# Sequence stage: four of 32 products with B moved from VectorE to GpSimd, their decays computed in place in PSUM

## What is computed

```
xi, z = split(seq @ in_proj)
xc    = silu(conv1d(xi) + b)
dt, Bm, Cm = split(xc @ x_proj);  dt = softplus(dt * dt_proj_w + dt_proj_b)
A   = -exp(A_log)
dA  = exp(dt[..., None] * A)
dBx = dt[..., None] * Bm[:, :, None, :] * xc[..., None]
h   = dA_t * h + dBx_t            (8 steps, h0 = 0)
y_t = sum_n h * C_t               ys + D * xc, times silu(z), then out_proj
```

## Time and profile before

| | us |
|---|---|
| median of three runs (10599.95 to 10654.83) | 10605.33 |
| the profiled execution | 10650.4 |
| its span | 10648.6 |
| VectorE busy in the span | 8923.8 (84%) |
| TensorE busy | 8596.3 (81%) |
| ScalarE busy | 6268.9 (59%) |
| GpSimd busy | 6010.0 (56%) |

### The profile page before, as it was taken

One profiled execution on the slowest core, in us unless ns is written; L12 is line 12 of the kernel. 1 busy time (PEld: TensorE's weight loads), 2 busy tenths in 40 slices (PEclk: granted clock), 3 DMA queues, 4 the chain that ended last, 5 costly groups with the idle time before them and its releaser, 6 DMA issues. The chain is left out here.

```text
span 10648.6 us, 196346 instructions
## 1 busy us (share of the span) xinstructions
PE 8596.3 (81%) x61658; PEld 3647.3 (34%) x61658; DVE 8923.8 (84%) x10968; ACT 6268.9 (59%) x11797; POOL 6010.0 (56%) x3646
## 2 busy tenths in 40 slices
PE   6999999989999997787877777877877777777760
PEld 3555555555555553222222222222222222222210
DVE  7777777777777775999999999999999999999984
ACT  5666666666666664555555555555555555555543
POOL 3222222222222221878878878787778878778760
PEclk9999999999999998888888888898888888888875
DMA  2223322232332321111111111111111111111129
GB/s 67 68 68 75 73 68 68 72 78 74 74 75 73 76 73 39 37 33 37 37 33 37 37 33 38 36 33 39 34 33 39 35 33 41 33 35 39 33 49 266
DMA packets 855791, 591.00 MB, mean 56 GB/s; under 512 B 621424, under 2 KB 725872, under 8 KB 848464
## 3 DMA queue, kind: packets, MB, share of 16 engines
q1 hardware_dynamic: 751440, 423.61, 17.3%
q0 software_dynamic: 49152, 100.76, 2.6%
q10 hardware_dynamic: 54016, 51.91, 1.6%
HBM read 109.27 MB, written 103.81 MB: 20 GB/s over the span
## 5 line engine op out<-in xcount | busy, mean ns | idle before, releaser
L1190 POOL TENSOR_TENSOR b_hh<-b_hh,b_cn 128x1024 f32<-128x1024 f32 x1600 | 3834.4, 2414 | 1053.3 <-DVE b_hh L1445 1052.9
L1445 DVE TENSOR_TENSOR_SCAN b_hh<-b_dA,b_ub 128x512 f32<-128x512 f32 x3200 | 3865.7, 1208 | 0.0
L1314 ACT ACTIVATE b_dA<-b_db,b_negA 128x448 f32<-128x448 f32 x3200 | 1980.6, 634 | 1761.4 <-PE b_db L1539 1755.4
L278 POOL DMA_DIRECT2D kvsel<-kv x1536 | 1104.2, 721 | 2877.1 <-issue 2456.0
L1437 DVE TENSOR_TENSOR b_ub<-b_ub,b_bn 128x512 f32<-128x512 f32 x3200 | 2174.8, 680 | 378.2 <-PE b_ub L1539 358.3
L1539 PE MATMUL b_ub<-b_rows,b_pick 96*64 96x512 bf16 x6400 | 1405.1, 440 | 1008.2 <-DVE b_hh L1445 949.8
L1539 PEld LDWEIGHTS b_ub<-b_rows,b_pick 96*64 96x64 bf16 x6400 | 359.1, 110 | 3194.7 <-DVE b_hh L1445 2535.5
L1539 PE MATMUL b_db<-b_rows,b_pick 96*64 96x512 bf16 x6400 | 1267.2, 419 | 218.7 <-ACT b_dA L1314 214.7
L554 DVE SCALAR_TENSOR_TENSOR oacc<-vpad,vec,oacc 128x1064 f32<-128x1064 f32 (+1 forms) x934 | 1199.4, 1301 | 11.4
L1575 PE MATMUL b_acc<-b_hh,b_gather 64*32 64x512 f32 x12800 | 1050.7, 719 | 2.8 <-POOL b_hh L1190 2.8
L395 ACT ACTIVATE prob<-score,nmax 128x256 f32<-128x256 f32 (+1 forms) x1600 | 737.4, 479 | 161.0 <-issue 91.3
(11 more groups left out here) (185 smaller groups left out, 12247.5 us busy)
## 6 DMA issues: line engine op xcount, KB each, us to landing
b_rows<-b_term SPq DMA_DIRECT2D x2400, 64.0 KB, 2.0
kvsel<-kv SPq DMA_DIRECT2D x1600, 64.0 KB, 2.1
kvsel<-kv POOLq DMA_DIRECT2D x1536, 64.0 KB
xpad<-in_x SPq DMA_DIRECT2D x18, 1568.0 KB, 10.7
ys<-ysb ACTq DMA_DIRECT2D x16, 1600.0 KB, 9.4
b_yc<-ys SPq DMA_DIRECT2D x100, 256.0 KB, 2.7
xr<-b_xo SPq DMA_DIRECT2D x100, 256.0 KB, 2.7
x<-x3pad SPq DMA_DIRECT2D x16, 1568.0 KB, 18.2
```

What stands on the lines that cost most here:

```text
L278: eng.dma_start(kvsel[:, slot, j, :, WPIX * t:WPIX * (t + 1)].unsqueeze(1), kv[:, bass.ds(at[t], 1), :, :]).then_inc((s_kv, s_kg)[j][slot] ...
L1190: nc.gpsimd.tensor_tensor(out=now, in0=now, in1=cn[:, par, :].unsqueeze(1).broadcast_to([C, 2, HT]), op=ALU.mult).then_inc(s_pm, 1)
L1314: nc.scalar.activation(later(dA[:, k % DEEP, :]), later(db[k % 2][:, :]), ACT.Exp, scale=negA[:, 8 * q + e:8 * q + e + 1]).then_inc(s_a, 1)
L1445: nc.vector.tensor_tensor_scan(hh[:, k // 2 % PDEEP, HT * (k % 2):HT * (k % 2 + 1)], dA[:, k % DEEP, :], ub[(UNITS * par + k) % 3][:, :], ...
```

## The change

Units 24, 26, 28 and 30 of each chunk are handled in another way (`AHEAD`). TensorE puts dt into their bank `ub` and u into `db`, the reverse of the others. ScalarE copies u from `db` to a place of the unit's own in SBUF (`su`), where GpSimd multiplies it with B (before pairs 8, 9, 10 and 11 of its products with C). ScalarE then makes the decay in place in PSUM: a copy of zeros into column t = 0 of `ub`, and an exponential over the other seven. These two stand in ScalarE's order after the decays of units 29, 31, 33 and 35 (the last two are units 1 and 3 of the next chunk). VectorE's scan of such a unit takes the rates from `ub` and the new terms from `su`, and has no product before it. The semaphore `bk` now counts 28 products in a chunk; `ex` and `sb` are new.

```diff
+        AHEAD = (24, 26, 28, 30)
+        PLAIN = UNITS - len(AHEAD)
+        su = sb("su", [C, len(AHEAD), HT])
...
+            def states_in(n, par, k):
+                pool.wait_ge(s_a, unit(n, k))
+                pool.wait_ge(s_bn, ONE + 2 * n + 1)
+                nc.gpsimd.tensor_tensor(out=own(k), in0=own(k), in1=bn[:, par, :], op=ALU.mult).then_inc(s_sb, 1)
...
                 for j in range(PAIRS):
+                    for k in AHEAD:
+                        if (k - 7) // 2 == j:
+                            states_in(n, par, k)
                     products(n, par, j)
...
             def decay(n, k):
                 act.wait_ge(s_dr, unit(n, k))
+                if k in AHEAD:
+                    if not is_first(n):
+                        act.wait_ge(s_sc, unit(n - 1, k))
+                    nc.scalar.activation(own(k), db[k % 2][:, :], ACT.Copy).then_inc(s_a, 1)
+                    return
...
+            def decay_in_place(n, par, k):
+                act.wait_ge(s_ur, unit(n, k))
+                q, e = channel(k)
+                here = ub[(UNITS * par + k) % 3][:, :]
+                nc.scalar.activation(first_of(here), first_of(dA[:, 0, :]), ACT.Copy)
+                nc.scalar.activation(later(here), later(here), ACT.Exp, scale=negA[:, 8 * q + e:8 * q + e + 1]
+                                     ).then_inc(s_ex, 1)
...
                 for k in range(28, 32):
                     decay(n, k)
+                    if k == 29:
+                        decay_in_place(n, par, 24)
+                    if k == 31:
+                        decay_in_place(n, par, 26)
                 if before_end(n, 2):
                     turned(n + 2)
                 if more:
-                    for k in range(UNITS, UNITS + LEAD):
+                    decay(n, UNITS)
+                    decay(n, UNITS + 1)
+                decay_in_place(n, par, 28)
+                if more:
+                    for k in range(UNITS + 2, UNITS + 4):
+                        decay(n, k)
+                decay_in_place(n, par, 30)
+                if more:
+                    for k in range(UNITS + 4, UNITS + LEAD):
                         decay(n, k)
...
             def recur(n, par, k):
-                dve.wait_ge(s_bk, unit(n, k))
-                dve.wait_ge(s_a, unit(n, k))
+                here = ub[(UNITS * par + k) % 3][:, :]
+                if k in AHEAD:
+                    dve.wait_ge(s_ex, ahead(n, k))
+                    dve.wait_ge(s_sb, ahead(n, k))
+                    rate, new = here, own(k)
+                else:
+                    dve.wait_ge(s_bk, plain(n, k))
+                    dve.wait_ge(s_a, unit(n, k))
+                    rate, new = dA[:, k % DEEP, :], here
...
-                    if k + 1 < UNITS or more:
+                    if k + 1 not in AHEAD and (k + 1 < UNITS or more):
                         states_in(n, par, k + 1)
                     recur(n, par, k)
...
-                repeat(ub[(UNITS * par + k) % 3], 1, par, k, s_ur)
+                repeat(ub[(UNITS * par + k) % 3], 0 if k in AHEAD else 1, par, k, s_ur)
...
-                repeat(db[k % 2], 0, par, k, s_dr)
+                repeat(db[k % 2], 1 if k in AHEAD else 0, par, k, s_dr)
```

More of the change, by code:

```diff
@@ L1050, in sequences @@
         s_sc = sem("sc")
+        s_ex = sem("ex")
+        s_sb = sem("sb")
         s_pm = sem("pm")
@@ L1077, in unit, with plain, ahead, own @@
             return ONE + UNITS * n + k + 1
+        def plain(n, k):
+            q, r = divmod(k, UNITS)
+            return ONE + PLAIN * n + PLAIN * q + len([x for x in range(r + 1) if x not in AHEAD])
+        def ahead(n, k):
+            return ONE + len(AHEAD) * n + AHEAD.index(k) + 1
+        def own(k):
+            return su[:, AHEAD.index(k), :]
         def pair(n, j):
@@ L1100, in later, with first_of @@
             return x.rearrange("c (m t) -> c m t", t=T)[:, :, 1:T]
+        def first_of(x):
+            return x.rearrange("c (m t) -> c m t", t=T)[:, :, 0:1]
         block = ctx.enter_context(nc.Block())
@@ L1130, in split @@
                     if r == 0 and not is_first(n):
-                        sp.wait_ge((s_dr, s_ur)[x], ONE + UNITS * n - UNITS)
+                        sp.wait_ge(s_dr, ONE + UNITS * n - UNITS)
+                        sp.wait_ge(s_ur, ONE + UNITS * n - UNITS)
                     for q in range(Q):
@@ L1295, in kept @@
                 if not early(n, 3):
-                    act.wait_ge((s_bk, s_pm)[x], ONE + (UNITS, PAIRS)[x] * n - 2 * (UNITS, PAIRS)[x])
+                    act.wait_ge((s_bk, s_pm)[x], ONE + (PLAIN, PAIRS)[x] * n - 2 * (PLAIN, PAIRS)[x])
+                    if x == 0:
+                        act.wait_ge(s_sb, ONE + len(AHEAD) * n - 2 * len(AHEAD))
                 nc.scalar.activation((bn, cn)[x][:, par, :], misc[:, :], ACT.Copy).then_inc(s_bn, 1)
@@ L1440, in recur @@
             def recur(n, par, k):
-                dve.wait_ge(s_bk, unit(n, k))
-                dve.wait_ge(s_a, unit(n, k))
+                here = ub[(UNITS * par + k) % 3][:, :]
[7 more added lines that the diff above has]
+                    rate, new = dA[:, k % DEEP, :], here
                 if k % 4 == 0 and not (is_first(n) and k // 2 < PDEEP):
                     dve.wait_ge(s_y, quad(n, (k // 2 - PDEEP) // 2))
-                nc.vector.tensor_tensor_scan(hh[:, k // 2 % PDEEP, HT * (k % 2):HT * (k % 2 + 1)], dA[:, k % DEEP, :],
-                                             ub[(UNITS * par + k) % 3][:, :], 0.0, ALU.mult, ALU.add
-                                             ).then_inc(s_sc, 1)
+                nc.vector.tensor_tensor_scan(hh[:, k // 2 % PDEEP, HT * (k % 2):HT * (k % 2 + 1)], rate, new, 0.0,
+                                             ALU.mult, ALU.add).then_inc(s_sc, 1)
             front(0)
```

## The result

| | before | after |
|---|---|---|
| median us | 10610.51 (4 runs) | 10546.53 (4 runs, 10544.08 to 10566.67) |
| ratio after / before, 95% interval | | 0.9936 [0.9918, 0.9955] |
| span of the profiled execution | 10648.6 | 10564.6 |
| mean granted clock | 0.898 | 0.899 |
| distance from the `gate` of one chunk to the next, mean of 93 chunks | 61.23 | 60.58 |

Ratios and medians leave out two timed executions that took over 17000 us, one of e9 and one of the kernel before beside e5 to e7.

The account below looks back on a forecast made before the run. VectorE was taken to bound the chunk as a whole, TensorE the stretch of units 24 to 30. 0.65 us x 100 chunks = 65 us gave about 10585 profiled, 10540 us as median; range 10430 to 10665.

Parts of the forecast that it names:

- TensorE is the bound from u25 to u31: In units 24 to 30 TensorE is as long as VectorE or longer, so the 2.32 us off VectorE mostly doesn't count.
- p31 and s30 come 0.65 us earlier on average: Behind u31, product 31 and scan 30 come forward 0.53, 0.67 and 0.75 us in three chunks, 65 us over 100 chunks.
- 1.67 us of new waiting per chunk: Of the 2.32 us VectorE saves per chunk in this stretch, 0.65 is gained and 1.67 becomes waiting.
- The in-place pair costs 0.72 us and delays `conv_even`: ScalarE's zero copy and exponential ahead of the yT copy take 0.72 us, delaying conv_even 0.01, 0.72, 0.25 us in three chunks.
- The scans at 1.21 us with rates from PSUM, the register instruction free, GpSimd covered: VectorE's four scans stay at 1.21 us, the added register instructions cost nothing, GpSimd's 4.8 us per chunk fits its waits.
- The rule against the change: Two-input elementwise work belongs on VectorE; alone it would make 4.8 us of GpSimd work for 2.3, set aside.
- The clock: TensorE's granted clock, left unchanged in the sum; rivals had it stay up more (17%) or fall once more per round (14%).
- the rivals: TensorE's clock stays up more, 106 us gained (17%), or falls once more per round, 86 us lost (14%).
- the first rival: TensorE's waits behind u31 shrink, so its clock falls less often: another 106 us gained, 10434 us, chance 17%.
- units 15 to 22: Units before u25 in which TensorE was called idle, given as evidence against the clock staying up more (17%).
- T's sums: Forecasts per run from the theory that TensorE's stretch from u25 to u31 sets when scan 30 can start.
- The prediction's sentence on the rule of the clock page: Idleness throttles TensorE and activity frees it; said to support the clock staying up more, 106 us, chance 17%.

Follow-up runs that it names:

- e9: Kernel before with units 22, 28 and 30 handled in the new way: 0.9787 of the kernel before, 10387.47 us.
- e5: Kernel before, no unit in the new way, transposes moved from s = 24 to 19, conv_even to 20, 21, 22, ScalarE's copies likewise: 0.9996 of the kernel before.
- e7: Changed kernel with only unit 30 handled in the new way: 0.9914 of the kernel before.
- e2: Changed kernel with only units 28 and 30 handled in the new way: 0.9879 of the kernel before.
- e8: Changed kernel with only unit 22 in the new way, its decay in place behind decay 27: 0.9954 of the kernel before.
- e3: Changed kernel with only units 24 and 26 handled in the new way: 0.9993 of the kernel before.
- e0: The changed kernel run again, no edit: 0.9945 of the kernel before.
- e1: Changed kernel with the copy to yT moved ahead of the decay in place of unit 26: 0.9890 of the kernel before.
- e6: Changed kernel with transposes, conv_even and ScalarE's two copies moved earlier as in e5: 0.9931 of the kernel before.
- e10: Units 20, 22, 28 and 30 in the new way, that is e9 plus unit 20: 0.9845 of the kernel before.
- e4b: Changed kernel with one more ScalarE copy of 512 columns just ahead of the copy to yT: 0.9934 of the kernel before.
- e11: The same kernel as e9 run again for a trace: 0.9798 of the kernel before, 10396.01 us.

## Why the prediction was right, point by point

- **TensorE is the bound from u25 to u31.** Right, and shown: products behind the stretch (e2, e7) or ahead of it (e8) count, those inside it (e3) do not, and this holds between chunks of like clock too.
- **p31 and s30 come 0.65 us earlier on average.** Right at like clock: 0.52 us where the level is low (0.53 was said for such a chunk) and 0.70 us at the middle clock (0.75 was said). Not so on average: in the trace of the change s30 comes 0.09 us earlier behind s22 than before, in that of e0 0.35 us, because the clock from u25 to u31 fell from 0.734 to 0.675 and 0.694. The mean chunk is 0.65 us shorter all the same, because the clock behind u31 rose, which gives 0.64 us. That the two came to the forecast is luck.
- **1.67 us of new waiting per chunk.** 170 us in the trace, but of two parts: VectorE's waits for units 24 to 31 grew by 2.3 us per chunk, and those further on fell by 0.6.
- **The in-place pair costs 0.72 us and delays `conv_even`.** 0.73 us measured. From u25 to u31 the delay is none at the lower level (14.25 us before and after; 0.01 was said) and 0.21 us at the middle clock (11.10 for 10.89; 0.25 was said). Moving the pair behind the copy (e1) brings some 60 us where 28 were priced; the rest goes with the clock (0.906 for 0.902).
- **The scans at 1.21 us with rates from PSUM, the register instruction free, GpSimd covered.** Right: 1212 ns; VectorE busy 54.9 us in a chunk (55.3 was said); 1268 ns per product of GpSimd where 1.2 us was taken, and the `add` hardly waits for it: TensorE waits 3.0 us for GpSimd in all.
- **The rule against the change** (the Trainium skill, GPSIMD Engine Reference, Engine selection): a product does take 1268 ns for 680 ns, a ratio of 1.9 where the page says about 2, and by it alone the change would lose. It does not, because GpSimd's waits fell by 557 us. The price shows in e6, where TensorE no longer covers it, and in e10, one product beyond e9: there GpSimd is the one waited for.
- **The clock.** The sum left it at zero, and the rivals had it gain 106 us or lose 86. Over the whole kernel zero is right (0.902 for 0.901 over the runs of e0). But both rivals' mechanisms are in the trace at once and cancel. The lower level comes more often in the stretch: 46 of 96 chunks have a clock under 0.7 from u25 to u31, where the kernel before had 27. And it comes less often behind u31, as the first rival said: 65 chunks have none of it there, where the kernel before had 27. In single chunks: the one at 4663.2 has u34 at 0.41 us where the third chunk of before ran it at 0.64, and is 57.10 us long for 59.30; the chunk at 4596.5 is 66.70 us for 63.10. A neutral sum is therefore luck.
- **A reading that was wrong.** The rival's "units 15 to 22" are not idle. In the first chunk TensorE waits 1.09 us for VectorE before u21, u23, u24 and u25 only, and is busy for 90% or more of the time from u13 to u20. The forecast does not use it.

Across the kernels the clock follows the difference from T's sums: e1, e2, e4b, e7 and e9 came out 20 to 70 us below them, with 0.905 to 0.916, and e5 some 80 above, with 0.894; e3, e8 and e0, with 0.902 to 0.904, within 10 us. e6 and e10 missed by more, and there GpSimd is waited for. That the products change nothing behind s30 at full clock is shown by the 20.26 us that the kernels have in common there. What moved the clock is not shown, for no run here sets it by itself. It goes with TensorE's wait before u32: where that is 0.85 to 0.99 us (before, e3, e5, e8) the clock behind it is 0.786 to 0.918, and where it is 0.10 to 0.35 us (after, e0, e1, e2, e4b, e7, e10, e11) 0.917 to 0.960; e6, with 0.39 us and 0.786, does not fit.

What stays open: why the clock falls in the chunks in which it does, and so which of two orders will be granted more. The prediction's sentence on the rule of the clock page (the Trainium skill, TensorE: Matmul & The Clock Gate, What's actually happening), that idleness throttles, agrees with the rows of e5 and of u25, where the lower level comes after steps in which TensorE waited for VectorE; no run tells how much waiting it takes.

## What to carry to other kernels

When an engine is the busiest on average, look at each piece of work that is to leave it and ask who is waited for there; four products, two of them at a place where another engine is the bound, brought hardly more at like clock (0.52 to 0.70 us) than the last of them alone (0.53 to 0.57), and less in the whole kernel's time. Place the moved work before or after such a stretch, and put nothing new on a queue in front of a copy on which the stretch waits: e9 does both and brings three times what the change does, part of it through the clock. Once an engine's slack has paid for some of the work, the next piece may come back through a third engine's queue, as unit 20 did through GpSimd and ScalarE.

## What the runs showed that I had not expected

A half microsecond put into every chunk (e4b), or 1.05 us taken out of one stretch of it (e5), left the time of the kernel where it was, and TensorE's granted clock had moved the other way: 0.910 and 0.894 after 0.902 and 0.900. The change itself gained at the place where the prediction looked and lost it there again to the clock; what remained came from behind it, where more chunks were granted the full clock. A change of some tenths of a per cent can't be read as the worth of a step in this stage unless chunks at the same clock are compared.

ScalarE writes an exponential of 448 columns in place in PSUM in 0.59 to 0.60 us, where PSUM to SBUF takes 0.63; the copy of 64 columns takes 0.28.
